# Norm scalars on POOL and ACT, and write vectors shifted one token by a transfer, in a two-layer kernel

## The reference

```
# layer 0 (cut)
xn = _layernorm(x)                       # over a token's 256 numbers
m  = _mamba_block(xn, ...)               # conv, selective scan over 1024 tokens, 16 states
c  = m + gelu(m @ ffn_w1.T + ffn_b1) @ ffn_w2.T + ffn_b2
mu, var = mean(c, axis=(1, 2)), var(c, axis=(1, 2))       # one per sequence
x  = x + (c - mu) / sqrt(var + EPS) + moe(xn)
# layer 1 (cut)
xn = _layernorm(x)
q, k, v = split(xn @ qkv_w + qkv_b)                       # 16 heads of 16, causal softmax
x_prev = concatenate([zeros(1 token), xn[:, :-1]])        # shifted by one token
w1, w2 = x_prev @ w1_write, xn @ w2_write                 # per head 4 numbers each
write_lines = exterior(w1, w2)                            # 6 differences w1_i w2_j - w1_j w2_i, normalized
read_lines  = exterior(xn @ w1_read, xn @ w2_read)
incidence   = einsum(read_lines, write_lines @ J)
mem_score   = sum_j(incidence**2 * decay**(i - j))        # j < i
gated = mean_h(sigmoid(mem_score * mem_scale) * sigmoid(xn @ memg_w + memg_b))
x = x + (seq_out + gated * (xn @ memv_w + memv_b)) @ out_w + out_b + lora_ffn(xn)
```

## Time and profile before

| | before |
|---|---|
| median of 3 runs | 3748.41 us (3742.24 to 3749.98) |
| the profiled execution's own time | 3745.62 us |
| its span, first to last instruction | 3743.9 us |
| granted TensorE clock, mean | 0.986 of full speed |
| PE / DVE / ACT / POOL busy | 95 / 85 / 71 / 61 % |

### The profile page before, as it was taken

How to read it: one execution, slowest core, us unless ns; L and a number is a source line. 1 busy time by engine, 2 the same in 40 slices (tenths; PEclk the granted TensorE clock), 3 DMA queues, 4 the chain that set the end, 5 groups by cost and what they waited for, 6 DMA issues and landing times.

```text
span 3743.9 us, 63558 instructions
## 1 busy us (share of the span) xinstructions
PE 3543.0 (95%) x20512; PEld 2364.9 (63%) x20512; DVE 3169.1 (85%) x6019; ACT 2654.0 (71%) x4087; POOL 2278.8 (61%) x1790
## 2 busy tenths in 40 slices
PE   7999999999999999999888999999999999999998
PEld 3666666656556665656665766767676676767665
DVE  3798999999999999999977688786968778696873
ACT  5878878788787878888634757566675757667565
POOL 3797999999999999999934142332514233251421
PEclk9999999999999999999898999999999999999999
DMA  4445445554554555545532123232312323231220
GB/s 155 134 162 166 161 148 181 155 170 163 167 167 148 177 166 166 170 149 178 191 97 97 42 78 101 70 109 70 115 48 81 98 70 115 64 122 48 75 84 21
DMA packets 253340, 456.88 MB, mean 122 GB/s; under 512 B 26116, under 2 KB 80852, under 8 KB 250196
## 3 DMA queue, kind: packets, MB, share of 16 engines
q1 hardware_dynamic: 253012, 452.82, 38.7%
HBM read 381.07 MB, written 69.21 MB: 120 GB/s over the span
## 4 chain that ended last, share of the span: by engine, by line
PE 50%; DVE 22%; issue 10%; ACT 8%; POOL 7%; DMA 2%; DVEq 0%; SPq 0%; POOLq 0%; ACTq 0%
DVE ps L2071 8%; PE ps L1661 6%; PE ps L1548 5%; PE ps L1653 5%; PE ps L1529 4%; POOL drive L2326 4%; PE ps L1511 3%; DVE heavy L2049 3%; ACT ps L1678 3%; PE ps L1413 3%; DVE held L2071 3%; PE ps L1463 2%; PE ps L1380 2%; ACT L1678 2%; PE ps L1588 2%
## 5 line engine op out<-in xcount | busy, mean ns | idle before, releaser
L2326 POOL TENSOR_TENSOR drive<-du,b_wide 128x1024 f32<-128x1024 f32 x512 | 1202.6, 2366 | 147.7 <-DVE held L2071 80.1
L1678 ACT ACTIVATE ps<-delta,neg_a 128x512 f32<-128x512 f32 x1024 | 684.4, 686 | 184.4 <-DVE heavy L2049 115.7
L1678 ACT ACTIVATE exps<-ps 128x1024 f32<-128x1024 f32 (+1 forms) x640 | 599.7, 939 | 228.9 <-PE ps L1529 224.9
L2360 POOL TENSOR_SCALAR_AFFINE_SELECT exps<-exps 128x256 f32<-128x256 f32 x512 | 204.4, 414 | 832.5 <-ACT exps L1678 832.5
L2094 DVE CUSTOM_DVE_ANT_0 ps<-ps,later 128x512 f32<-128x512 f32 (+3 forms) x1024 | 474.6, 518 | 55.1 <-PE ps L1511 53.1
L2049 DVE TENSOR_TENSOR heavy<-c_wide,ps 128x512 f32<-128x512 f32 x704 | 450.5, 676 | 15.2 <-issue 14.1
L1463 PEld LDWEIGHTS ps<-p_all,heavy 128*128 128x128 f32 x3072 | 355.2, 142 | 152.5 <-issue 76.9
L2071 DVE TENSOR_TENSOR_SCAN ps<-ps,carry,drive 128x512 f32<-128x512 f32 x352 | 434.8, 1274 | 10.6 <-ACT ps L1678 10.6
L1463 PE MATMUL ps<-p_all,heavy 128*128 128x128 f32 x3072 | 415.0, 277 | 23.3 <-DVE heavy L2049 20.8
L2071 DVE TENSOR_TENSOR_SCAN ps<-ps,drive 128x512 f32<-128x512 f32 x352 | 414.0, 1215 | 25.3 <-ACT ps L1678 21.9
L2310 POOL TENSOR_TENSOR held<-held,c_wide 128x1024 f32<-128x1024 f32 x160 | 378.4, 2365 | 6.4
(11 more groups left out here) (212 smaller groups left out, 7175.2 us busy)
## 6 DMA issues: line engine op xcount, KB each, us to landing
b_wide<-bc_dram SPq DMA_DIRECT2D x512, 256.0 KB, 3.4
c_wide<-bc_dram SPq DMA_DIRECT2D x512, 256.0 KB, 3.6
stacks<-parts SPq DMA_DIRECT2D x192, 256.0 KB, 2.5
qs<-stacks SPq DMA_DIRECT2D x128, 192.0 KB
ks<-stacks SPq DMA_DIRECT2D x128, 192.0 KB, 4.4
x_row<-in_x SPq DMA_DIRECT2D x14, 1024.0 KB, 7.9
resid<-mix SPq DMA_DIRECT2D x9, 1024.0 KB, 5.5
x_row<-resid SPq DMA_DIRECT2D x9, 1024.0 KB, 6.1
```

The costliest lines, as they stand in the source:

```text
L1678: return nc.scalar.activation(out_, in_, func, **kw)
L2326: G.tensor_tensor(drive[:, g % DRIVE_SLOTS, :, :], du[:, e, :, :], wide(b_wide[:, g % B_SLOTS, :], MD), ALU.mult).then_inc(driven, 1)
```

## The change

It has three parts. In layer 0 "offset" goes from DVE to POOL; "square" becomes one instruction of ACT (Identity, with a scale and a bias from `row_q` and `row_mv`) where it was two of DVE; "shift" becomes one of ACT (Copy with a scale) where it was one of DVE.

In layer 1 "pb" is one product of 320 columns from unshifted tokens, six matmuls where twelve stood. ACT drains its 64 columns into a new tile `ahead` [128, 9, 64], by token and tile, whose first slot it fills with zeros once a sequence. A new task "shift" of SP, once for each half, moves them into `pt1` one token on: partitions 0 to 126 to 1 to 127 in one transfer, and partition 127 of the tiles before to partition 0 in a second. POOL's "outer" waits for both (`shifted`), and they wait for the four `outer` of the half before (`outer_done`). The zero columns of `xT` and their two memsets are no longer needed.

Third, lengths, `SHIFTS`, `RUN` and `STAY` have new values, so that the order is a new one on all engines.

```diff
-            add("v", ("offset", b), 0.14, at + NT, ("v", "scale", b))
+            add("g", ("offset", b), 0.15, at + NT, ("v", "scale", b))
...
-LENGTH = {"xt": 0.44, "qk": 1.40, "pa": 1.28, "pb": 1.40, "lt": 0.44, ...
+LENGTH = {"xt": 0.44, "qk": 1.40, "pa": 1.28, "pb": 0.92, "lt": 0.44, ...
...
-                add("g", ("outer", b, t), 1.05, place["pb", b, t], ("a", "pb", b, t),
+                if t % TC == TC - 1:
+                    add("s", ("shift", b, c), 0.8, place["pb", b, t], ("a", "pb", b, t),
+                        ("g", "outer", (n - TC) // NT, (n - TC) % NT) if n >= TC else None, late=2.2)
+            for t in range(TC * c, TC * (c + 1)):
+                n = NT * b + t
+                add("g", ("outer", b, t), 1.05, place["pb", b, t], ("s", "shift", b, c),
...
-SHORT, RUN, STAY = 0, 1, 0.03
+SHORT, RUN, STAY = 0, 3, 0.02
...
-    ("a", 1): {"logistic": 44, "length": 31, "qk": 11, "pa": 9, "pb": 23, "st": 5, "turn": -20},
+    ("a", 1): {"logistic": 83, "length": 39, "f1": -17, "gelu": 1},
...
+                elif kind == "shift":
+                    c = task[2]
+                    drained(sp, plan, ("pb", n, TC * c + TC - 1), "a")
+                    sp.wait_ge(ahead_set, n + 1)
+                    if NC * n + c:
+                        sp.wait_ge(outer_done, TC * (NC * n + c))
+                    sp.dma_start(pt1[1:P, :, 0:64], ahead[0:P - 1, TC * c + 1:TC * (c + 1) + 1, :]).then_inc(shifted, 16)
+                    sp.dma_start(pt1[0:1, :, 0:64], ahead[P - 1:P, TC * c:TC * (c + 1), :]).then_inc(shifted, 16)
...
                     for n, (k, by, of) in enumerate(three):
-                        mm(bank[:, 0:D], xT[of][:, k, tokens(t)], w[by][:, k, 0:D], start=(n == 0),
-                           stop=(n == len(three) - 1), skip_group_check=True)
-                    for n, (k, by, of) in enumerate(three):
-                        last = mm(bank[:, D:D + 64], xT[of][:, k, tokens(t, shift=0)], w[by][:, k, D:D + 64],
-                                  start=(n == 0), stop=(n == len(three) - 1), skip_group_check=True)
+                        last = mm(bank[:, 0:D + 64], xT[of][:, k, tokens(t)], w[by][:, k, :], start=(n == 0),
+                                  stop=(n == len(three) - 1))
...
+                elif kind == "square":
+                    act.wait_ge(row_apart, j + 1)
+                    f(row_q[:, 1:2], row_q[:, 4:5], ACT.Identity, scale=row_q[:, 4:5], bias=row_mv[:, 1:2]).then_inc(row_square, 1)
+                elif kind == "shift":
+                    drained(act, L0_PLAN, ("mu", j), "v")
+                    act.wait_ge(row_inverse, j + 1)
+                    f(row_q[:, 2:3], row_q[:, 0:1], ACT.Copy, scale=row_q[:, 3:4]).then_inc(row_shift, 1)
...
+                    if t == 0:
+                        if n:
+                            act.wait_ge(shifted, 32 * NC * n)
+                        f(ahead[:, 0, :], ident[:, 0:64], ACT.Copy, scale=0.0).then_inc(ahead_set, 1)
...
-                    f(pt1[:, task[2] % TC, 0:64], full(act, plan, task)[:, D:D + 64], ACT.Copy).then_inc(drained_a, 1)
+                    bank = full(act, plan, task)
+                    if n:
+                        act.wait_ge(shifted, 32 * NC * n)
+                    f(ahead[:, task[2] + 1, :], bank[:, D:D + 64], ACT.Copy).then_inc(drained_a, 1)
...
-                elif kind == "offset":
-                    dve.wait_ge(scale_done, parts_done(b, part))
-                    own = tiles_of(b, part)
-                    dve.wait_ge(minus_done, parts_done(b, part))
-                    V.tensor_tensor(ln_shift[:, own], ln_minus[:, own], ln_rstd[:, own], ALU.mult).then_inc(offset_done, 1)
...
-                elif kind == "square":
-                    dve.wait_ge(row_apart, 2 * b + 1)
-                    V.tensor_tensor(row_q[:, 5:6], row_q[:, 4:5], row_q[:, 4:5], ALU.mult).then_inc(row_apart, 1)
-                    dve.wait_ge(row_apart, 2 * b + 2)
-                    V.tensor_tensor(row_q[:, 1:2], row_q[:, 5:6], row_mv[:, 1:2], ALU.add).then_inc(row_square, 1)
...
-                    V.tensor_tensor(row_q[:, 2:3], row_q[:, 0:1], row_q[:, 3:4], ALU.mult).then_inc(row_shift, 1)
...
+                if kind == "offset":
+                    own = tiles_of(j, i)
+                    pool.wait_ge(scale_done, parts_done(j, i))
+                    pool.wait_ge(minus_done, parts_done(j, i))
+                    pool.wait_ge(norm_done, NT * j)
+                    G.tensor_tensor(ln_shift[:, own], ln_minus[:, own], ln_rstd[:, own], ALU.mult).then_inc(offset_done, 1)
...
                     drained(pool, plan, ("pb", n, t), "a")
+                    pool.wait_ge(shifted, 32 * (NC * n + t // TC + 1))
```

More of the change, by code:

```diff
@@ L320, in layer0_tasks @@
             "mu": lambda: [("v", "gather", j)],
-            "var": lambda: [("v", "square", j)]}[kind]()
+            "var": lambda: [("a", "square", j)]}[kind]()
         empties = {
@@ L327, in layer0_tasks @@
             "o": lambda: [("s", "keep", j // NC - 1) if j else ("s", "first")] if j % NC == 0 and last == 0 else [],
-            "mu": lambda: [("v", "square", j - 1), ("v", "shift", j - 1)],
+            "mu": lambda: [("a", "square", j - 1), ("a", "shift", j - 1)],
             "var": lambda: [("a", "centre", j - 1)]}.get(kind, list)()
@@ L345, in layer0_tasks @@
             if j % NC == NC - 1 and last == TC - 1:
-                add("v", ("gather", j // NC), 0.2, start + 4, ("v", "spread", j, last), ("v", "square", j // NC - 1))
+                add("v", ("gather", j // NC), 0.2, start + 4, ("v", "spread", j, last), ("a", "square", j // NC - 1))
         elif kind == "mu":
-            add("v", ("square", j), 0.35, start + 3, ("v",) + unit)
+            add("a", ("square", j), 0.25, start + 3, ("v",) + unit)
         elif kind == "var":
@@ L656 @@
 TURN, DRIFT = 0.1, 0.042
-SHORT, RUN, STAY = 0, 1, 0.03
+SHORT, RUN, STAY = 0, 3, 0.02
 PULL = {"a": 0.016, "v": 0, "g": 0, "s": 0.0}
 SHIFTS = {
[3 rows of a table removed]
-    ("g", 0): {"drive": 6, "weigh": 5, "du": 13, "join": 4.8},
[6 rows of a table removed]
-    ("v", 0): {"scan": 43, "weigh": -39, "stats": 14.4},
-    ("v", 1): {"gate": 42, "wo": -12, "bias": 34, "mt": 6, "sm": 1.9, "ot": -22, "xt": 18, "lines": 14, "normal": 19},
+    ("a", 0): {"xt": -22.4, "res": 22, "skip": 19, "decay": 4, "gelu": 12, "soft": 32, "root": 33, "norm": 3.6,
+        "xd": -34, "mh": 3.5, "m": -5, "xm": -6, "gelu_t": 18, "centre": -8, "shift": -3.3, "silu_x": -5},
+    ("a", 1): {"logistic": 83, "length": 39, "f1": -17, "gelu": 1},
+    ("g", 0): {"drive": 2, "join": -2, "weigh": -16, "offset": -11},
+    ("g", 1): {"feat_w": -35, "outer": -19},
[5 rows of a table added]
+    ("v", 0): {"scan": 45, "spreads": 21, "stats": 6, "weigh": -12},
+    ("v", 1): {"gate": 48, "sm": 3, "mt": 17, "ot": -19, "ms": 13, "unit": 15, "lines": 5, "bias": 42, "pa": 13},
 }
@@ L931, in build @@
         zero_rows = rows[80:82, 0, :]
-        pt1, pt2, outer, lines, norm, feat_w, feat_r, gsum, lines_at = place(
-            body_at, ("pt1", [P, TC, 2 * 4 * H]), ("pt2", [P, TC, 2 * 4 * H]), ("outer", [P, 2, 2 * H, 4, 4]),
+        pt1, pt2, ahead, outer, lines, norm, feat_w, feat_r, gsum, lines_at = place(
+            body_at, ("pt1", [P, TC, 2 * 4 * H]), ("pt2", [P, TC, 2 * 4 * H]), ("ahead", [P, NT + 1, 64]), ("outer", [P, 2, 2 * H, 4, 4]),
             ("lines", [P, 2, TC, 2 * H, 6]), ("norm", [P, TC * 2 * H]), ("feat_w", [P, TC, NPQ * H]),
@@ L1048, in build @@
         outer_done = sem("outer_done")
+        ahead_set = sem("ahead_set")
+        shifted = sem("shifted")
         lines_read = sem("lines_read")
@@ L2030, in _ @@
                     row_task(("stats", 0, t))
-                for kind in ("spreads", "scale", "offset"):
+                for kind in ("spreads", "scale"):
                     row_task((kind, 0, part))
@@ L2124, in attention_task @@
                     drained(dve, L0_PLAN, ("dl", NH - 1, MI - 1), "a")
-                    for one in xT:
-                        V.memset(one[:, :, 0:1].bitcast(F32), 0.0).then_inc(setup1_v, 1)
                     V.tensor_tensor(param("outb"), param("outb"), param("gb2"), ALU.add).then_inc(setup1_v, 1)
@@ L2314, in _ @@
             G.memset(const[:, 1:2], float(H)).then_inc(consts_set, 1)
+            for part in range(NC):
+                row_task(("offset", 0, part))
             row_task(("du", 0, 0))
```

31 lines of the change are left out of this document (13 added, 18 removed), and 13 rows, old and new, of the table SHIFTS.

## The result

The changed kernel takes 3856.23 us (median of 4 runs, 3854.96 to 3862.24), beside 3746.45 for the kernel before (3742.24 to 3749.98): a ratio of 1.0297, 95 % interval 1.0279 to 1.0314. It is 111 us slower, where 3738 was forecast and 3795 was the upper end. The forecast was wrong in size and sign; the rival that ends on the slower side, a landing later than 9.3 us, had the right side and a third of the size.

The account below looks back on a forecast made before the run. DVE was taken to pace layer 0, with PE and POOL close behind, and PE layer 1. −27 − 24 + 38 + 4 = −9 us against 3745.6 gave 3737, stated as 3738; range 3685 to 3795.

Parts of the forecast that it names:

- Term 1: Layer 0: moving norm scalars off DVE frees 31.4 us, of which 0.87 is credited: −27 us.
- Term 2: Layer 1's write product: six 320-column matmuls for twelve save 31 us of PE work, −24 us counted.
- weak bound: The smallest gain allowed for the 320-column product in layer 1: −12 us, against −31 at the other end.
- Term 3: Layer 1's token-shift transfer: one engine, landing in 8.7 us; DVE stands 8.5 us a batch, PE loses 5.5: +38 us.
- The fixed part: Layer 1's transfer: time besides moving bytes, 1.7 us, with 0.3 more for the second piece.
- the cover: Layer 1: banks filled and emptied ahead spare PE 3 us a batch of DVE's standing still.
- The +4 for the bunched order: Layer 1: DVE's lines held beside a running `outer` on POOL, some 28 us of DVE time, cost +4 us.
- C: Rival for layer 1's transfer: each 256-byte piece costs 20 ns, landing after 11.9 us; 3782 us, chance 0.24.
- D: Rival: layer 0 doesn't follow DVE, or both layers' other order costs what the scalars give; 3764 us, chance 0.10.

Follow-up runs that it names:

- scalars, lists kept: Kernel before with only the norm scalars moved to POOL and ACT, every other list order as before: 3724.18 us, ratio 0.9956.
- product, lists kept: Kernel before with scalars moved and the 320-column product, old lists, token shift left out, no transfer: 3718.05 us, ratio 0.9926.
- new lists, no transfer: Changed kernel without any transfer: ACT drains the 64 columns straight into pt1, token shift left out: 3754.64 us, ratio 1.0037.
- three pieces: Changed kernel with the 127-partition transfer issued as two, over 112 and 15 partitions, beside the one for partition 0: 3764.61 us, ratio 1.0060.
- the slots: Changed kernel with eight slots for pt1 and seven for pt2 in place of four each: 3858.02 us, ratio 1.0291; with the transfer in pieces, 3762.03 us.
- the half-width run: Changed kernel with 32 of the 64 columns through the single transfer, the rest drained straight into pt1 unshifted: 3809.59 us, one execution.

## Why the prediction was wrong

By ratios, each difference within some 0.2 % (8 us), of 3746 us; the steps are rounded, and unrounded they add up to 111:

| step | us | predicted |
|---|---|---|
| scalars, lists kept (0.9956) | −16 | −27 |
| product, lists kept (0.9926) | −11 | −24 |
| new lists, no transfer (1.0037) | +42 | +4 |
| three pieces (1.0060) | +9 | |
| one piece over 127 partitions (1.0297) | +89 | +38 |
| sum | +111 | −9 |

**Term 1** was right in its mechanism: layer 0 ends 22 us earlier with the old lists. 0.87 of the 31.4 us of DVE time was too much: 0.70 arrives at the end of layer 0 and 0.53 in the whole. In the changed kernel only 9 us of it are left, since the new lists take 12 in layer 0.

**Term 2** was right in the spacing (0.15 us) and too high twice. It took six spacings for a tile's product, 0.90 us, and 1.06 was measured, so the work saved is 21 us and not 31. And of these only −11 and −12 arrive, at or just past the weak bound: PE's idle time takes up the rest even where nothing else changes.

**Term 3, the step that failed.** "One engine" and its rate were right, and so was DVE's standing still (6.14 against 5.5, 10.0 a sequence against 8.5). The fixed part was 1.6 us too small. What failed is the sentence "PE feels less: a bank or so is filled and emptied ahead in each half, ... 3 us a batch". Of DVE's 10.0 us PE feels 9.0 as idle time (18.8 us a sequence against 9.8 in the same lists without a transfer): the cover is 1 us and not 3. And then it works at the lower clock, which I didn't count at all: 3.2 us more of the transfer's. That makes 12.2 us a sequence where 5.5 were forecast. And I left out ACT's and POOL's stops as "free in the same moment". That was right for ACT, as the slots showed, but POOL's masks held PE for 4.8 us in the second half.

**The +4 for the bunched order** was the second failure, by a factor of ten. I priced the lines that are held by `outer`, DVE's 4 us a sequence; and DVE's busy time did rise, by 5.8 us in the changed kernel and by 3.7 without the transfer. The larger cost lies in what PE waits for while POOL and DVE work off a half's `outer` and lines in one piece: the bunching alone, in the old lists, takes 60 us with 2.7 us more of DVE's time a sequence. The new lists, bunched too, lose 42, so the search may have won some back. Some 8 of the 42 lie in layer 0, where nothing is bunched: without the transfer its last products of C start at 1889.2 us, and at 1880.7 with both gains in the old lists. How the rest is split between bunching and the other differences of the lists stays open, since no plan with other lengths is comparable.

**The rivals.** C named the right mechanism, the landing, with the wrong reason: the half-width run shows bytes, and leaves at most 7 ns for a piece where C had 20. Its formula, with a landing of 10.0, would have given 3755 us. The range left out the case in which the cover is missing and the clock falls. D had "the other order of both layers costs what the scalars give" and came to +18 us; the order's 42 are that case in a larger size.
